# Mixing tables of the three conditional layers: one matmul on 24 stacked high and low rows where there was an fp32 matmul on 8 rows

## What is computed

```
h = jax.nn.gelu(embedding @ W0 + b0, approximate=False)
h = jax.nn.gelu(h @ W1 + b1, approximate=False)
att = jax.nn.softmax((h @ W2 + b2) / T, axis=-1)
agg_w = jnp.einsum('bk,koi->boi', att, weight[..., 0])
agg_b = att @ bias_k
out = jnp.einsum('boi,bih->boh', agg_w, x) + agg_b[:, :, None]
```

## Time and profile before

| what | value |
| --- | --- |
| device time, median of 3 executions | 801.61 us (799.82 to 804.09) |
| the profiled execution | 802.86 us, its span 801.1 us |
| PE busy | 752.3 us, 94% of the span, 3631 matmuls |
| PE weight loads | 607.2 us, 76% |
| DVE, ACT, POOL busy | 478.7 us (60%), 274.9 us (34%), 416.2 us (52%) |
| mean granted PE clock | 0.973 |

### The profile page before, as it was taken

One profiled execution on the slowest core, in us unless ns is written; L12 is line 12 of the kernel. 1 busy time (PEld: TensorE's weight loads), 2 busy tenths in 40 slices (PEclk: granted clock), 3 DMA queues, 4 the chain that ended last, 5 costly groups with the idle time before them and its releaser, 6 DMA issues. The chain is left out here.

```text
span 801.1 us, 11113 instructions
## 1 busy us (share of the span) xinstructions
PE 752.3 (94%) x3631; PEld 607.2 (76%) x3631; DVE 478.7 (60%) x1038; ACT 274.9 (34%) x531; POOL 416.2 (52%) x450
## 2 busy tenths in 40 slices
PE   5999999999999999999999999988899889999993
PEld 4487777777688888888888878766787767878782
DVE  1557766668623255745575358863788877666541
ACT  5334444444422243422424243312432232222220
POOL 2386667775425341112311057685578767687840
PEclk9689999999999999999999999999899999999997
DMA  9346555644051031110321024136031121212110
GB/s 268 60 93 172 158 159 181 175 132 133 27 183 53 27 87 59 54 28 1 111 86 28 1 79 158 54 83 195 2 117 56 53 67 41 64 56 70 51 40 13
DMA packets 49223, 69.60 MB, mean 87 GB/s; under 512 B 25816, under 2 KB 26072, under 8 KB 48904
## 3 DMA queue, kind: packets, MB, share of 16 engines
q1 hardware_dynamic: 39424, 38.52, 16.3%
q0 software_dynamic: 9232, 29.96, 12.3%
q10 hardware_dynamic: 512, 0.41, 0.2%
HBM read 45.71 MB, written 17.66 MB: 79 GB/s over the span
## 5 line engine op out<-in xcount | busy, mean ns | idle before, releaser
L1475 DVE TENSOR_TENSOR sil<-bank,sil 128x512 f32<-128x512 f32 x56 | 38.6, 690 | 96.6 <-PE bank L1969 96.6
L1969 PE MATMUL bank<-th,wgr 128*128 128x512 f32 x224 | 88.3, 394 | 2.4 <-POOL tl L552 1.8
L1828 PE MATMUL bank<-wda,hh 128*128 128x512 f32 x224 | 89.2, 398 | 0.0
L1920 PE MATMUL bank<-wda,xch 128*128 (+1 forms) x272 | 86.3, 399 | 2.3 <-DVE xcl L1500 2.3
L1828 PE MATMUL bank<-wda,hl 128*128 128x512 f32 x224 | 88.3, 394 | 0.0
L1969 PE MATMUL bank<-th,wur 128*128 128x512 f32 x224 | 87.4, 390 | 0.0
L1969 PE MATMUL bank<-tl,wgr 128*128 128x512 f32 x224 | 87.2, 389 | 0.0
L1969 PE MATMUL bank<-tl,wur 128*128 128x512 f32 x224 | 87.2, 389 | 0.0
L1036 ACT ACTIVATE hh<-sil 128x512 fp32r<-128x512 f32 x56 | 35.4, 632 | 107.6 <-DVE sil L1475 107.6
L1477 DVE TENSOR_TENSOR hl<-sil,hh 128x512 fp32r<-128x512 f32 x56 | 45.1, 806 | 39.1 <-ACT hh L1036 39.1
L1028 ACT ACTIVATE sil<-bank 128x512 f32<-128x512 f32 x56 | 33.4, 597 | 100.4 <-PE bank L1969 100.4
(11 more groups left out here) (324 smaller groups left out, 1887.7 us busy)
## 6 DMA issues: line engine op xcount, KB each, us to landing
tap<-in_x_taps_dram SPq DMA_DIRECT2D x16, 260.0 KB, 2.8
xin<-in_x_rows_dram SPq DMA_DIRECT2D x16, 256.0 KB, 3.1
xd<-xo SPq DMA_DIRECT2D x16, 256.0 KB, 3.2
xc<-xd SPq DMA_DIRECT2D x16, 256.0 KB, 3.4
xres<-xd SPq DMA_DIRECT2D x4, 1024.0 KB, 5.5
xd<-xres SPq DMA_DIRECT2D x4, 1024.0 KB, 4.7
tsd<-tf SPq DMA_DIRECT2D x4, 1024.0 KB, 4.5
raw<-in_w_dram POOLq DMA_DIRECT2D x16, 256.0 KB, 3.1
```

Of the source, the lines that this page charges most:

```text
L1475: v.tensor_tensor(hf[:, m % 2], p_pre[(2 * m + 1) % 3][:], sil[:, m % 2], ALU.mult).then_inc(s_hf, 1)
L1828: last = mm(p_acc[j][:], h[:, m % HSLOTS, j * P:(j + 1) * P], wda[:, m * D:(m + 1) * D], start=(m == 0 and n == 0), stop=(m == MT - 1 and ...
L1920: last = mm(bank[(p + 1) % 2][:], x, y, start=(k == 0 and n == 0), stop=(k == KT - 1 and n == 2))
L1969: last = mm(p_pre[(2 * m + b) % 3][:], w[:, (m * KT + kt) * P:(m * KT + kt + 1) * P], x[:, kt], start=(kt == 0 and n == 0), stop=(kt == KT ...
```

## The change

The tables come from fp32r matmuls. The softmax (`att3`, 64 x 3 layers x 3 x 8) holds its high part twice and its low part once, and is transposed to 24 rows (`attt`). The ingredients (`mix3`, 24 rows) hold the high part in rows 0 to 7 and 16 to 23 and the low part in rows 8 to 15, so that one matmul over 24 rows gives high x high + high x low + low x high. POOL makes the high part (three new instructions on 8 x 1056) and sends it to rows 16 to 23 by a transfer; DVE makes the low part `mixl` (three new instructions), and POOL sends it to rows 8 to 15 by a second transfer. `mixb` lies in the last 32 columns of `mixw`. Besides, the work at the start is put in another order: PE makes the scores behind router(0), and conv(1) stands before mixing_weights and mixed(0); ACT makes tap_hi(1) behind hid2 and t0_hi(0).

```diff
+            mix3 = sb("mix3", [3 * MIX, COND_LAYERS, AGB], F32R, st)
...
+            sp.dma_start(mixw[:, :, 0:AGW], mix_w).then_inc(d_mix, 16)
+            sp.dma_start(mixw[:, :, AGW:AGB], mix_b).then_inc(d_mix, 16)
...
             tap_lo(0)
+            pool.wait_ge(d_mix, 32)
+            for l in range(COND_LAYERS):
+                nc.gpsimd.tensor_scalar(mix3[0:MIX, l], mixw[:, l], 1.0, 1.0, ALU.mult, ALU.mult).then_inc(s_mixh, 1)
+            pool.wait_ge(s_mixh, COND_LAYERS)
+            pool.dma_start(mix3[2 * MIX:3 * MIX], mix3[0:MIX]).then_inc(d_mst, 16)
             tap_lo(1)
+            pool.wait_ge(s_mixl, COND_LAYERS)
+            pool.dma_start(mix3[MIX:2 * MIX], mixl[:]).then_inc(d_mst, 16)
             pool.wait_ge(s_lbs, 1)
...
             conv_out(0)
-            tap_hi(1)
-            act.wait_ge(s_m2, COND_LAYERS)
+            act.wait_ge(s_m1, 2 * COND_LAYERS + 1)
...
             t0_hi(0)
+            tap_hi(1)
...
+            for l in range(COND_LAYERS):
+                dve.wait_ge(s_mixh, l + 1)
+                v.tensor_tensor(mixl[:, l], mixw[:, l], mix3[0:MIX, l].bitcast(F32), ALU.subtract).then_inc(s_mixl, 1)
             t0_lo(0)
...
-            v.tensor_tensor(att[:], atte[:], rows(2), ALU.mult).then_inc(s_at, 1)
+            chain.link(v.tensor_tensor(att[:], atte[:], rows(2), ALU.mult))
+            chain.link(v.tensor_copy(att3[:, :, 0], att[:]))
+            v.tensor_copy(att3[:, :, 1], att3[:, :, 0].bitcast(F32))
+            v.tensor_tensor(att3[:, :, 2], att[:], att3[:, :, 0].bitcast(F32), ALU.subtract).then_inc(s_at, 1)
...
-            pe.wait_ge(s_g2, COND_LAYERS)
-            for l in range(COND_LAYERS):
-                last = mm(bank[4][0:BATCH, l * MIX:(l + 1) * MIX], hid2[:, l], mw2[:, l], start=True, stop=True)
-            last.then_inc(s_m2, 1)
+            def scores():
+
+                pe.wait_ge(s_g2, COND_LAYERS)
+                for l in range(COND_LAYERS):
+                    last = mm(bank[4][0:BATCH, l * MIX:(l + 1) * MIX], hid2[:, l], mw2[:, l], start=True, stop=True)
+                last.then_inc(s_m1, 1)
...
-                pe.wait_ge(d_mix, 32)
+                pe.wait_ge(d_mst, 32)
...
-                mm(bank[5][0:BATCH, :], attt[:, l], mixw[:, l, 0:512], start=True, stop=True)
-                mm(bank[6][0:BATCH, :], attt[:, l], mixw[:, l, 512:AGW], start=True, stop=True).then_inc(s_ag, 1)
+                mm(bank[5][0:BATCH, :], attt[:, l], mix3[:, l, 0:512], start=True, stop=True)
+                mm(bank[6][0:BATCH, :], attt[:, l], mix3[:, l, 512:AGW], start=True, stop=True).then_inc(s_ag, 1)
...
                 router(t)
                 if t == 0:
+                    scores()
+                if t + 1 < TILES:
+                    conv(t + 1)
+                if t == 0:
                     mixing_weights()
                     mixed(0)
-                if t + 1 < TILES:
-                    conv(t + 1)
                 base(t)
```

More of the change, by code:

```diff
@@ L144, in build @@
             mb2 = sb("mb2", [BATCH, COND_LAYERS, MIX], F32, st)
-            mixw = sb("mixw", [MIX, COND_LAYERS, AGW], F32, st)
-            mixb = sb("mixb", [MIX, COND_LAYERS, CH], F32, st)
+            mixw = sb("mixw", [MIX, COND_LAYERS, AGB], F32, st)
             hid1 = sb("hid1", [P, COND_LAYERS, BATCH], F32, st)
@@ L151, in build @@
             attm = sb("attm", [BATCH, 3, COND_LAYERS], F32, st)
-            attt = sb("attt", [MIX, COND_LAYERS, BATCH], F32, st)
+            att3 = sb("att3", [BATCH, COND_LAYERS, 3, MIX], F32R, st)
+            attt = sb("attt", [3 * MIX, COND_LAYERS, BATCH], F32R, st)
+            with ExitStack() as st2:
+                mixl = sb("mixl", [MIX, COND_LAYERS, AGB], F32R, st2)
             aggs = sb("aggs", [BATCH, COND_LAYERS, AGB], F32, st)
+            mix3 = sb("mix3", [3 * MIX, COND_LAYERS, AGB], F32R, st)
             wsc = sb("wsc", [P, 3, KT], F32, st)
@@ L273, in build @@
             sem(f"d_{n}") for n in "cond mlp mix conv ga w0 lb w1 l3".split())
+        s_mixh, s_mixl, d_mst = (sem(f"{n}") for n in "s_mixh s_mixl d_mst".split())
         d_sw, d_swb, d_agg, d_tab, d_b1b = (sem(f"d_{n}") for n in "sw swb agg tab b1b".split())
@@ L277, in build @@
         s_cvw, s_gas, s_w0s, s_w0l, s_lbs = (sem(f"s_{n}") for n in "cvw gas w0s w0l lbs".split())
-        s_bias, s_m1, s_g1, s_m2, s_g2, s_lm, s_ex, s_at, s_att, s_atc, s_mb, s_ag, s_agc = (
-            sem(f"s_{n}") for n in "bias m1 g1 m2 g2 lm ex at att atc mb ag agc".split())
+        s_bias, s_m1, s_g1, s_g2, s_ex, s_at, s_att, s_atc, s_ag, s_agc = (
+            sem(f"s_{n}") for n in "bias m1 g1 g2 ex at att atc ag agc".split())
         s_sw, s_wqf, s_wqr, s_wqt, s_wqc = (sem(f"s_{n}") for n in "sw wqf wqr wqt wqc".split())
@@ L857, in _ @@
                 nc.scalar.activation(w0h[:, k], w0_raw[:, k], ACT.Copy).then_inc(s_w0s, 1)
-            act.wait_ge(s_lm, 1)
+            act.wait_ge(s_at, 1)
             nc.scalar.activation(atte[:], att[:], ACT.Exp).then_inc(s_ex, 1)
@@ L862, in _ @@
             act.wait_ge(s_att, 1)
-            nc.scalar.activation(attt[:].rearrange("k l b -> k (l b)"), bank[5][0:MIX, 0:COND_LAYERS * BATCH],
+            nc.scalar.activation(attt[:].rearrange("k l b -> k (l b)"), bank[5][0:3 * MIX, 0:COND_LAYERS * BATCH],
                                  ACT.Copy).then_inc(s_atc, 1)
@@ L870, in mixed @@
                 act.wait_ge(s_ag, l + 1)
-                act.wait_ge(s_mb, 1)
+                act.wait_ge(s_att, 2)
                 nc.scalar.activation(aggs[:, l, 0:512], bank[5][0:BATCH, :], ACT.Copy).then_inc(s_agc, 1)
@@ L1123, in _ @@
             chain.link(v.tensor_reduce(attm[:, 0, :], att[:], AX.X, ALU.max))
-            v.tensor_tensor(att[:], att[:], rows(0), ALU.subtract).then_inc(s_lm, 1)
+            v.tensor_tensor(att[:], att[:], rows(0), ALU.subtract).then_inc(s_at, 1)
             dve.wait_ge(s_ex, 1)
```

15 lines of the change are left out of this document (7 added, 8 removed).

## The result

The changed kernel took 812.66 us (median of 6 executions, 811.24 to 815.45), the kernel before 801.79 us on the same chip (median of 6): a ratio of 1.0137, 95% interval 1.0111 to 1.0164, or +10.9 us (8.9 to 13.1). On a second chip the ratio was 1.0124 (1.0097 to 1.0152). Forecast were +6.9 us and 808.5 us, with a range up to 812.5: the direction is right, the size is 4 us short, and the time lies 0.2 us above the range. The profiled execution of the changed kernel took 811.41 us, its span 809.7 us.

The account below looks back on a forecast made before the run. The prediction took the chain of the mixing tables, ending in `bd1l` before mix1(0), to bound the kernel; +5.0 for mix1(0) and +1.9 for the clock gave +6.9 on 801.61, 808.5 us, range 802.0 to 812.5.

Parts of the forecast that it names:

- Router(0), +4.1 by the sum: Start of stage 1: high parts on POOL and low parts on DVE take turns before `t0l`; router(0) 4.1 us later, at 21.75.
- the row at 23.83: Earlier trace, DVE: a tiny subtraction took 1.87 us, held until POOL's `lbl` was done; basis for assuming holding.
- that at 45.12: Earlier trace, DVE: the same instruction took 0.16 us beside POOL's `wq_rows`, not held; would put router(0) at 18.35.
- From router(0) to the end of mixed(0), 9.8: PE, stage 1: 9.8 us instead of 8.8, as conv(1) and the scores come before the cheaper mixing; 1.0 more.
- d: Shift of mixed(0)'s end, said to move the whole chain of the tables equally: 4.1 + 1.0 = 5.1 us.
- A: Rival, DVE between `gal` and `t0l`: DVE not held or `mixw` early; d 1.75, 803.8 us; chance 0.29.
- B: Rival, PE: matmuls save in full since PE's own chain ends last, not the tables; -4.9, 796.7 us; chance 0.08.
- C: Rival, mixing: the stack is late or one pass no cheaper; mixed(0) ends 2.9 later, 811.4 us; chance 0.08.
- the second transfer: Transfer into `mix3`: lands at 29.4, needed at 30.3; hidden, costs nothing, with 0.9 us to spare.
- mix1(0) 56.1: First matmul using the mixing tables, on PE: starts at 56.1 instead of 51.1, +5.0 us.
- The clock, +1.9: PE's wait before `weights_t` and behind it: the clock falls to 0.50 and costs 1.9 us, bounds 0 and 3.1.
- ends about d - 0.1 later: Whole kernel: if mixed(0) ends d later, the end moves by about d - 0.1, however much PE saves on the way.

Follow-up runs that it names:

- x_after_code: The changed kernel with 9 more matmuls of 32 columns on PE, result unused, behind the transposes of tile 0; ratio 1.0098 to the kernel before.
- x_after_pause: The changed kernel with POOL writing zeros twice (about 1.1 us, overwritten at once) before its third late weight split; ratio 1.0109 to the kernel before.
- x_pool_split: The changed kernel with two of POOL's four quantising pieces put ahead of its first `bd1f`; 808.61 us, ratio 1.0058 to the kernel before.
- x_fill: The changed kernel with 22 more matmuls of 512 columns on PE, result unused, ahead of `weights_t`; 811.02 us, ratio 1.0082 to the kernel before.
- x_both_split: The changed kernel with both old orders (DVE, PE) and two of POOL's four quantising pieces ahead of its first `bd1f`; ratio 1.0023 to the kernel before.
- x_dve_order: The changed kernel with the three `mixl` subtractions behind t0_lo(0) on DVE; 808.82 us, ratio 1.0066 to the kernel before.
- x_both_orders: The changed kernel with low parts behind t0_lo(0) on DVE and PE's mixing ahead of conv(1), fp32r mixing kept; 808.17 us, ratio 1.0072 to the kernel before.

## Why the prediction was right in stage 1 and short in all

- **Router(0), +4.1 by the sum: 3.66 measured** (4.0 if counted from the end of `gal`), from the same mechanism: POOL's high parts and DVE's low parts held each other, with `mixw` landing at 12.83 where 12.5 was assumed. The choice between the row at 23.83 and that at 45.12 was right: long instructions held each other. That the sum fits so well is in part luck. The forecast had six turns of 1.27 us from the end of `gal` (7.6 us) and left tap_lo(1) out; measured were six turns of 0.93 to 1.12 and tap_lo(1) (`tapl`, 1.30 at 18.20) between them, ahead of the last low part's end, 7.5 us together. By the rule of the Trainium skill (SBUF — State Buffer, section Who interferes with whom) router(0) was to start at 21.75, and it started at 21.28.
- **From router(0) to the end of mixed(0), 9.8: 10.1 measured** (21.28 to 31.41). conv(1) as cover for the softmax, one pass for each product, 1.4 us for the mixing: as worked out. d was 5.1, measured 5.0. But the chain behind it didn't move by all of d, as the forecast said: `bd1f` came 4.35 us later, for 0.7 us were made up in the read-back of the tables. Rivals A, B and C fall; the second transfer was hidden.
- **mix1(0) 56.1: 55.46**, with PE idle for 5.40 us before `weights_t` (6 forecast) and POOL's `wq_rows` as what ended it.
- **The clock, +1.9: 0.7 to 1.1.** The fall came where it was forecast, but `weights_t` (1.8 us at the slow clock, 0.9 before) lay wholly under the wait for `bd1l`, which ended at 55.36. Stage 1 in all: 6.9 forecast, 5.1 and 5.3 measured in the two profiles.
- **The step that failed is the sentence that the kernel "ends about d - 0.1 later" and the sum that goes with it.** It had no term behind mix1(0), on the ground that PE is busy without a gap from 50 us on, for which it had a row of 50 to 60 us only the earlier trace rows. PE isn't: it waits for DVE at 505 us (1.26 us before, 2.51 changed), and DVE and POOL decide how long. The profile of before had that row, and I didn't read it. In the two profiles of the changed kernel this added 1.3 us, clock stretches behind it 0.9 and 3.7 us net, and in one of them the slow stretch at 208 us 1.3 us: +8.6 and +10.3 us at the end. The 2.3 us between +8.6 and +10.9 are in neither profile of that pair: before's profiled execution lay 1.1 us above its median, the changed kernel's 1.3 below. Only the 1.3 us at 505 are shown, by x_after_code and x_after_pause, to come from the change; for the clock stretches the cause stays open.
- **What stays open**: what decides whether DVE or POOL is held (x_pool_split), why the clock falls at 208 us in some executions (the changed kernel, x_fill, x_both_split) and not in others with the same wait of PE there (x_dve_order, 1.42 us), and how much of the slow stretches at 506, 566 and 630 us belongs to the change. They vary by 3 us from one execution of the changed kernel to the other.

## What to carry to other kernels

An engine that is 94% busy has few waits, and each of them decides: list them all, over the whole span, before a sum is called complete, and ask of each whether the place of two engines' instructions against each other sets it. A change in the number of an engine's instructions also moves where its code is loaded, so a result of 1 to 2 us can come from a place a few hundred microseconds away from the edit; a control with the same instruction count, or the same lateness without the edit, tells the two apart. And a cheaper step pays only when what waits behind it is cheap too: here a kernel with fp32r mixing ended 10.9 us later than before in one order, and 2.8 us earlier in another, with POOL's work split and the code load put back.

## What was new about the hardware

- Code is loaded by DMA in packets of 16 KB, 31 in a run with 3631 matmuls on record (queue q8), and one of them took about 1 us (489.01 to 490.07). The transfer of 256 KB that it met landed after 4.0 to 4.6 us and not after 3.1 to 3.3.
- Rows of only 8 partitions don't shorten an instruction of DVE or POOL, nor keep them from holding each other: a subtraction of 1056 elements on 8 rows took 1.24 us where POOL did nothing beside it, and 1008 elements on 128 rows took 1.21. The three took 6.58 us beside POOL's high parts and `tapl`, 4.79 when they began behind the high parts and only `tapl` was beside them (x_both_orders).
- The hold isn't a matter of share: the same 128 x 512 instruction took 0.69, 0.98, 1.31, 1.65 or 1.77 us by its place against POOL's, and the pattern repeated to 0.02 us in many of the kernels; x_pool_split, with nearly the same distance at one place, went the other way (1.50).
